# Ranks and picked rows ahead of the bucket sums: an order of work on TensorE in a graph layer with a scatter

## The reference

```
h   = relu(layernorm(x)) @ W_in2f.T                       # per node
Wij = (smu(edge_attr @ W_f1.T + b_f1) @ W_f2.T + b_f2) * edge_weight
agg = segment_sum(h[dst] * Wij, src)                      # src is in no order
out = x + smu(agg @ W_o1.T + b_o1) @ W_o2.T + b_o2
```

## Time and profile before

| | us |
|---|---|
| median of 3 runs | 4155.02 (4153.83 to 4162.68) |
| the profiled execution | 4145.66 |
| its span | 4143.9 |

### The profile page before, as it was taken

The page is one execution under the profiler, slowest core; times in us unless marked ns, Lnnn a source line. Parts: engine busy times, 40 slices in busy tenths (PEclk is TensorE's granted clock), DMA queues, the critical chain, the costliest instruction groups (busy, mean ns, idle before and its releaser), DMA issues.

```text
span 4143.9 us, 90305 instructions
## 1 busy us (share of the span) xinstructions
PE 3504.1 (85%) x19070; PEld 2324.8 (56%) x19070; DVE 3785.0 (91%) x13416; ACT 2194.0 (53%) x7302; POOL 3050.2 (74%) x3173
## 2 busy tenths in 40 slices
PE   6677768888888888888888899988889989998889
PEld 2344335555555555555555566665556666665658
DVE  8889779998999889999899999999999999999997
ACT  4677555555555555555555555555555545455543
POOL 4777777777777777777777777777777767777772
PEclk9999999999999999999999999999999999999999
DMA  7566656666666555665555666666656776765658
GB/s 210 151 172 186 166 146 182 189 188 187 186 172 163 163 161 159 166 164 162 159 160 164 174 187 191 189 187 176 168 167 184 202 189 196 204 190 169 182 163 237
DMA packets 459534, 736.87 MB, mean 178 GB/s; under 512 B 87168, under 2 KB 255466, under 8 KB 459104
## 3 DMA queue, kind: packets, MB, share of 16 engines
q1 hardware_dynamic: 291606, 461.44, 44.7%
q0 software_dynamic: 100000, 206.60, 14.4%
q10 hardware_dynamic: 67626, 65.48, 4.8%
HBM read 465.36 MB, written 267.82 MB: 177 GB/s over the span
## 4 chain that ended last, share of the span: by engine, by line
POOL 25%; DVE 23%; issue 20%; DMA 14%; PE 13%; ACT 2%; ACTq 1%; POOLq 1%; DVEq 0%; SPq 0%
POOL sorted_rows L590 25%; DMA sorted_rows<-msg,row_idx 14%; DVE product L1012 5%; DVE seg_hot L1038 4%; DVE hg L1004 3%; PE p_w L1219 3%; DVE act L981 3%; DVE onehot L990 3%; PE p_seg L1264 3%; PE p_h L1234 2%; PE p_m L1225 2%; PE p_z L1214 1%; DVE pair_hot L996 1%; DVE pick L985 1%; DVE row_idx L1023 1%
## 5 line engine op out<-in xcount | busy, mean ns | idle before, releaser
L590 POOL DMA_INDIRECT sorted_rows<-msg,row_idx x3125 | 3009.3, 963 | 1017.1 <-issue 913.8
L725 ACT ACTIVATE msg<-p_m,weight 128x128 f32<-128x128 f32 x3136 | 896.2, 369 | 1136.2 <-PE p_m L1225 1121.4
L1264 PEld LDWEIGHTS p_seg<-seg_hot,seg 128*128 128x128 f32 x8288 | 1028.4, 192 | 323.4 <-issue 321.6
L1264 PE MATMUL p_seg<-seg_hot,seg 128*128 128x112 f32 x8288 | 1027.5, 274 | 15.0 <-issue 8.1
L1225 PE MATMUL p_m<-ident,hg 128*128 128x128 f32 x3136 | 516.5, 288 | 571.6 <-DVE hg L1004 568.1
L1012 DVE CUSTOM_DVE_ANT_0 product<-onehot,p_pos,start_at 128x112 bf16<-128x112 bf16 x3136 | 853.0, 328 | 9.1 <-PE p_pos L1253 4.3
L1219 PE MATMUL p_w<-act,w_f 128*128 128x512 f32 x1568 | 828.9, 611 | 4.2 <-DVE act L981 4.2
L1214 PE MATMUL p_z<-attr,w_f 128*128 128x512 f32 x1568 | 819.5, 605 | 14.3 <-DMA attr<-in_attrT 9.4
L1225 PEld LDWEIGHTS p_m<-ident,hg 128*128 128x128 f32 x3136 | 339.7, 143 | 796.5 <-DVE hg L1004 646.9
L709 ACT ACTIVATE gelu<-p_z 128x512 f32<-128x512 f32 x784 | 469.3, 599 | 460.4 <-PE p_z L1214 455.8
L1234 PE MATMUL p_h<-pick,win 128*128 128x512 bf16 x2352 | 654.4, 388 | 1.1 <-DMA win<-h 1.1
(11 more groups left out here) (116 smaller groups left out, 2242.3 us busy)
## 6 DMA issues: line engine op xcount, KB each, us to landing
seg<-sorted_rows SPq DMA_DIRECT2D x448, 322.5 KB
seg<-sorted_rows SPq DMA_DIRECT2D x196, 516.0 KB
ends<-ends SPq DMA_DIRECT2D x392, 256.0 KB
sorted_rows<-msg,row_idx POOLq DMA_INDIRECT x3125
sorted_rows<-zero_rows ACTq DMA_DIRECT2D x336, 129.0 KB
win<-h SPq DMA_DIRECT2D x392, 96.0 KB
attr<-in_attrT SPq DMA_DIRECT2D x392, 80.0 KB
seg<-sorted_rows SPq DMA_DIRECT2D x56, 387.0 KB
```

What stands on the lines that cost most here:

```text
L590: pool.indirect_dma_start(out=sorted_rows[:, :], out_offset=bass.IndirectOffsetOnAxis(ap=row_idx[:, slot, k:k + 1], axis=0), in_=msg[:, sl ...
L725: last = act.activation(msg[:, slot, k, 0:F], p_m[:, k, :], ACT.Copy, scale=weight[:, bass.ds(n.value(TILES_U, k), 1)])
L1264: last = pe.matmul(out, seg[:, it.slot, l * it.tiles + k, 0:F], seg_hot[:, it.slot, l * it.tiles + k, :], start=(k == 0), stop=(k == it.ti ...
```

## The change

In TensorE's step `rank` and `targets` of unit c-1 move from behind `turn` of unit c-2 to the place right behind `filter1` of unit c; the bucket sums, `turn` and `filter2` follow. In ScalarE's step `take_targets` of unit c-1 and `limits` of unit c (limits and start values for the places) move ahead of `keys` and `weigh` of unit c-2. The first two steps of the run are written out apart and stay as they are.

```diff
@@ ScalarE, step
+                if st.has(1):
+                    take_targets(st.at(1), st.v(1))
+                if st.has(0):
+                    if st.chunk() is not None:
+                        act.wait_ge(s_prep, PREPS * (st.chunk() + 1))
+                    limits(st.at(), st.ring(), st.rnd)
                 if st.chunk(2):
                     act.wait_ge(s_prep, PREPS * (st.chunk(2) + 1))
                     if st.chunk(2) == 1:
...
                 if st.has(2):
                     keys(st.at(2), st.ring(2), st.rnd_of(2))
                     weigh(st.at(2), st.ring(2))
-                if st.has(1):
-                    take_targets(st.at(1), st.v(1))
-                if st.has(0):
-                    if st.chunk() is not None:
-                        act.wait_ge(s_prep, PREPS * (st.chunk() + 1))
-                    limits(st.at(), st.ring(), st.rnd)
@@ TensorE, step
                 if st.has():
                     filter1(st.at(), st.pair(), st.q(), st.v())
+                if st.has(1):
+                    rank(st.at(1), st.ring(1), st.rnd_of(1), st.opens(1))
+                    targets(st.at(1), st.pair(1), st.q(1), st.v(1))
                 for it in st.items(1):
                     bucket_sum(it)
                 if st.has(2):
                     turn(st.at(2), st.v(2))
                 if st.has(1):
-                    rank(st.at(1), st.ring(1), st.rnd_of(1), st.opens(1))
-                    targets(st.at(1), st.pair(1), st.q(1), st.v(1))
                     filter2(st.at(1), st.v(1))
```

## The result

The changed kernel takes 4196.26 us in the median (4193.52 to 4199.34, 5 runs), the kernel before 4157.99 beside it (4153.83 to 4163.40): a ratio of 1.0089 (95% interval 1.0078 to 1.0100), 37 us slower. I had forecast slower, by 20 us, with a range up to 4193. The sign was right, and so were the openings as one place of the loss; a second place, the dense steps, I had put at almost nothing, and the size was wrong.

What follows compares the result with a forecast made beforehand. POOL was taken to bound the middle, VectorE the stretch from about unit 664. 18.1 + 4.8 - 1.9 - 1.5 + 0.8 = 20.3 us gave 4166 on the profiled execution's scale, 4175 on the median's; range 4157 to 4193.

Steps and rivals of the forecast that it cites:

- the openings: The nine steps that open a round, where ranks wait for VectorE's counts; forecast to lose time by order and clock.
- the dense steps: Steps with 8 to 12 tiles: p_w some 0.8 us later, an offset paid once from unit 664 on, +0.8 us.
- The bound, and what releases POOL: POOL's scatters bound the middle, 1.263 us each; scatters of unit n wait for p_w of unit n+2.
- Ordinary steps: Steps that open no round: p_w 0.2 us later against 3.2 us of slack; taken as 0, bounds -3 and +5.
- The openings' D: Delay of p_w at openings, as bucket sum and transposes come behind the wait for counts; loss 18.1 us, bounds 0 and 21.
- The clock: TensorE's longer idle at openings brings half clock behind it; 0.6 us at each of eight, 4.8 us, ends 0 and 14.
- Rival (d): At openings, every lengthened idle costs the full 1.7 us of half clock: 4184 us; chance 0.66 together with the forecast.
- rival (c): TensorE becomes the bound in dense stretches (units 448 to 528, 664 to 712): 38 us, 4193 or 4213; chance 0.06.
- Where it helps: Where VectorE's product is late, ranks are done already: -1.9 us at 262.00, -1.5 after the late scatter at 3412.30.

Runs made afterwards that it cites:

- open_clock_3: The changed kernel with 28 transposes of the identity keeping TensorE busy in the wait for counts at each opening step; ratio 1.0061 to the kernel before.
- open_old_3: The changed kernel with only the nine steps that open a round put back to the old order on TensorE; ratio 1.0033 to the kernel before.
- open_new_3: The kernel before with only the nine opening steps in TensorE's new order; ratio 1.0070, and 1.0017 as open_new on a chip where the kernel before took 5217 to 5220 us.
- early_pair_3: The changed kernel with SyncE's attr and ends loads issued one step earlier, ahead of the bucket load; ratio 1.0060 to the kernel before.
- before_again: The kernel before, unchanged, run again for a second trace; ratio 1.0002, profiled span 4149.4 us.

## Why the prediction was wrong in size

- **The bound, and what releases POOL.** Right. 1.26 us from scatter to scatter stayed, and POOL's longer idles explain the span.
- **Ordinary steps cost nothing.** Right for one item a step: units 224 to 336 take 5.095 us a step against 5.064, and of these 3.5 us the opening at the end is 2.8. Wrong where a step has more: see the dense steps below.
- **The openings' D (18.1 us).** Right in the mechanism and in the sum. The nine D add up to 20.0 (the bound of 21 in the forecast is a slip). At full clock p_w came later by 15.8 us in all (open_clock_3), since a tile costs 0.22 us there, not 0.248: with 5, 8, 10 and 12 tiles there are 3.3, 4.0, 4.4 and 4.9 us from seeds to the end of p_w, against 1.8 before. POOL stood 14.7 us longer, where I had 18.1; single openings were off by up to 1.5 us both ways, so the nearness of the sum is in part luck.
- **The clock (4.8 us, from ends of 0 and 14).** The term of the sum that was mis-sized. All nine waits (2.85 to 4.02 us) ended at or beside a granted clock of 0.50, and it made p_w 15.7 us later, 1.7 an opening; in time, open_clock_3 gave back 12 us. The rows of before gave 1.7 us as the price of one such stretch, and I took 0.6 because the slow p_w of the earlier trace rows had cost 0.47. But the half clock falls on the row of work behind the wait (sum, transposes, p_w), not on the p_w alone. Rival (d), 4184, was nearer than the forecast. The Trainium skill's warning of idle gaps (TensorE: Matmul & The Clock Gate, "Why this matters for your kernels") agrees with the nine idles of this trace. Openings in all: 23 us (open_old_3) to 29 (open_new_3), where forecast and clock gave 22.9.
- **The dense steps (0.8 us).** The step that failed. I had costed them as an offset of p_w, and set the later bucket load at 0, "over two steps ahead of its use". I looked at when the load is used, and not at what stands behind it in SyncE's order. There attr and ends were held back, and POOL stood 24.7 us longer over the dense steps (28.4 in place of 3.7), the largest single error. Taking the loads out from behind it gave back 17.7 of these, and 12 us of time (early_pair_3, whose openings were 4 us longer). The load is issued late; it is not a DMA that takes long, and rival (c), which put the bound on TensorE, can have at most the remaining 7.
- **Where it helps (-3.4).** Right in part. POOL's wait for the late landing at unit 661 is 5.24 us over the usual in place of 6.70: 1.5, as worked out, and it is 4.9 to 5.7 in every prompt trace with ranks ahead, 6.7 to 7.3 in the four without. The idle at 262 is gone, but that proves nothing: it is missing in before_again as well. Over all steps outside openings and dense stretches POOL's idle fell from 23.3 (26.4 in before_again) to 17.8 us, so the term was too small by 2 to 5 us.
- **The sum, mended.** By POOL's idles between the two traces: openings 31.4, dense steps 24.7, the rest -5.5, together 50.6 us for a span 47.9 longer. By time: the openings in the old order gave back 23 us, loads that come earlier 12, both together all but 1 of the 37 (1.0003). What is open: these times come from different chips, with intervals of 5 to 7 us to either side, so a difference of two of them is known to some 8 us (an estimate from the intervals), and the parting between openings and loads is no sharper than that.

## What to carry to other kernels

When work moves behind a wait that comes once in many steps, cost that step by itself: there it loses the cover that it had, and where it follows an idle of the engine (2.85 to 4.02 us here), price the work behind the wait at half clock too, not one instruction of it (here 33 of 49 us). When a consumer is moved, look at each queue that waits for it to free a buffer, and at everything that stands behind that entry in the queue. Then take the change apart: the place of the ranks was worth 9 us (0.9978, 4141.95 against 4150.66) once the sums kept theirs and nine steps of 784 kept the old order.

## What the hardware showed that I had not expected

- 28 matmuls whose result is thrown away, put in nine waits, made the kernel 12 us faster, by the clock alone (granted clock 1.00 in 1165 to 1177, in place of 0.50).
- On two chips the kernel before ran 25% longer, in every run (the changed one 23%). In a step of open_new, TensorE's ranks, transposes and p_w had ended by 2006.1, and VectorE, ScalarE and POOL, waiting for one each, went on within 1 us of each other only at 2009.14 to 2010.01 (the profile calls the releaser "remote", having no record of it):

```profile
2003.88 0.60 PE L1225 MATMUL p_m<-ident,hg 128*128 128x128 f32 x4
2004.36 0.21 PE L1253 MATMUL p_pos<-unit_hot,before 128*128 128x112 bf16 x1
2005.06 1.02 PE L1219 MATMUL p_w<-act,w_f 128*128 128x512 f32 x2
...
2009.14 0.33 DVE L1012 CUSTOM_DVE_ANT_0 product<-onehot,p_pos,start_at 128x112 bf16<-128x112 bf16 x1 [3.52 <-remote]
2009.19 1.14 ACT L725 ACTIVATE msg<-p_m,weight 128x128 f32<-128x128 f32 x4 [5.55 <-remote]
...
2010.01 0.96 POOL L590 DMA_INDIRECT sorted_rows<-msg,row_idx  x1 [2.74 <-remote]
```

What holds them back is not shown by any trace here. It was not seen on the two other chips, where the later runs were made; whether it belongs to the chip or to the time was not tested.
